# Gate and up of the FFN as seven block products for two batches, on one core

## What is computed

```python
x = L0_attn_hidden_states
x = x + attention(layernorm(x), w_attn, b_attn, w_proj, b_proj)
h = layernorm(x)
gate = silu(einsum('bsh,ih->bsi', h, w_gate))
up = einsum('bsh,ih->bsi', h, w_up)
return x + einsum('bsi,hi->bsh', gate * up, w_down)
```

## Time and profile before

| | |
|---|---|
| Median of 3 runs | 869.31 us (867.79 to 871.29) |
| Profiled execution | 872.76 us |
| Its span, first to last instruction | 871.1 us |
| Mean granted TensorE clock | 0.982 |
| Busy in the span | TensorE 816.1, VectorE 500.6, ScalarE 357.6, GpSimd 187.4 us |
| `ffn`, first matmul to end | 516.4 to 871.1 us |

### The profile page before, as it was taken

One profiled execution on the slowest core, in us unless ns is written; L12 is line 12 of the kernel. 1 busy time (PEld: TensorE's weight loads), 2 busy tenths in 40 slices (PEclk: granted clock), 3 DMA queues, 4 the chain that ended last, 5 costly groups with the idle time before them and its releaser, 6 DMA issues. The chain is left out here.

```text
span 871.1 us, 13365 instructions
## 1 busy us (share of the span) xinstructions
PE 816.1 (94%) x4576; PEld 563.4 (65%) x4576; DVE 500.6 (57%) x1539; ACT 357.6 (41%) x693; POOL 187.4 (22%) x336
## 2 busy tenths in 40 slices
PE   3889898999999999999978989999999999999998
PEld 3645365555555565565624668887888788878886
DVE  6598687887988779887784444342222312232223
ACT  4336566665666655666566323231111211121111
POOL 5224233343433424434234200000000000000000
PEclk9999899999999999999988989999999999999999
DMA  8864447565665556655642246004000400030001
GB/s 272 236 204 143 143 157 218 161 196 161 203 189 179 168 178 206 203 179 169 222 155 89 104 140 246 13 1 146 0 1 1 144 0 0 0 135 9 0 0 48
DMA packets 70563, 109.31 MB, mean 125 GB/s; under 512 B 13395, under 2 KB 38662, under 8 KB 70505
## 3 DMA queue, kind: packets, MB, share of 16 engines
q1 hardware_dynamic: 68457, 108.32, 38.9%
q10 hardware_dynamic: 2048, 0.27, 0.2%
HBM read 65.97 MB, written 42.32 MB: 124 GB/s over the span
## 5 line engine op out<-in xcount | busy, mean ns | idle before, releaser
L909 DVE CUSTOM_DVE_ANT_0 bank<-bank,mask_qk 128x512 f32<-128x512 f32 (+3 forms) x512 | 240.4, 514 | 56.3 <-PE bank L1148 53.9
L741 ACT ACTIVATE pt<-bank 128x512 f32<-128x512 f32 (+1 forms) x384 | 194.2, 529 | 136.9 <-PE bank L1170 123.3
L1170 PE MATMUL bank<-q_st,k_st 116*128 116x512 bf16 (+3 forms) x512 | 135.4, 308 | 15.9 <-ACT pt L741 13.2
L1148 PE MATMUL bank<-k_st,q_st 97*128 97x512 bf16 (+3 forms) x512 | 133.2, 311 | 10.8 <-DMA q_st<-slopes_dram 4.8
L1487 DVE TENSOR_TENSOR gu<-bank,silu 128x512 f32<-128x512 f32 x40 | 27.7, 692 | 200.6 <-issue 121.1
L1148 PEld LDWEIGHTS bank<-k_st,q_st 97*128 97x128 bf16 x512 | 41.5, 99 | 79.7 <-issue 39.9
L1265 PE MATMUL bank<-fT_hi,wgu_hi 128*128 128x512 f32 x224 | 88.5, 395 | 4.1 <-DVE wgu_lo L1457 4.1
L1265 PE MATMUL bank<-fT_lo,wgu_hi 128*128 128x512 f32 x224 | 88.2, 394 | 0.0
L1265 PE MATMUL bank<-fT_hi,wgu_lo 128*128 128x512 f32 x224 | 88.1, 393 | 0.0
L1420 ACT ACTIVATE silu<-bank 128x512 f32<-128x512 f32 x40 | 24.0, 600 | 148.2 <-PE bank L1265 148.2
L646 POOL TENSOR_SCALAR_AFFINE_SELECT pt<-pt 128x256 f32<-128x256 f32 x128 | 56.5, 442 | 129.7 <-ACT pt L741 129.7
(11 more groups left out here) (106 smaller groups left out, 1396.6 us busy)
## 6 DMA issues: line engine op xcount, KB each, us to landing
stack_dram<-scratch SPq DMA_DIRECT2D x32, 384.0 KB, 3.1
q_st<-stack_dram SPq DMA_DIRECT2D x32, 384.0 KB
k_st<-stack_dram SPq DMA_DIRECT2D x32, 384.0 KB
stack_dram<-scratch SPq DMA_DIRECT2D x32, 256.0 KB, 3.5
pv_dram<-weighed SPq DMA_DIRECT2D x32, 256.0 KB, 4.4
weighed<-pv_dram SPq DMA_DIRECT2D x17, 256.0 KB
xt<-x SPq DMA_DIRECT2D x16, 256.0 KB, 3.6
stack_dram<-scratch SPq DMA_DIRECT2D x32, 128.0 KB, 4.2
```

The costliest lines, as they stand in the source:

```text
L741: act.activation(pt[:, h % PT_RING, COL0[k]:COL0[k] + WIDE[k]], bank[3 + (3 * h + k) % 2][:, 0:WIDE[k]], ACT.Exp, scale=1.0 / HD).then_inc ...
L909: last = dve.tensor_tensor_reduce(bank[k][:, at:at + n], bank[k][:, at:at + n], mask_qk[:, S - n:S], 1.0, NEG, ALU.add, ALU.max, mx[:, h % ...
L1148: last = pe.matmul(bank[k][:, at:at + n], q_st[0:K_MAX, s, h % 4, t * P:(t + 1) * P], k_st[0:K_MAX, s, h % 4, 0:n], start=True, stop=True)
L1170: last = pe.matmul(bank[3 + u % 2][:, at:at + n], k_st[0:K_EXP, s, h % 4, t * P:(t + 1) * P], q_st[0:K_EXP, s, h % 4, t * P:S], start=True ...
```

## The change

Gate and up of one block for two batches are a product of 2x2 blocks: the weights' rows are gate and up, their columns the two halves of the contraction (A11, A12: gate; A21, A22: up), the tokens' rows the two halves, their columns the even and the odd batch (0 and 1, then 2 and 3). Eight block products become seven, by Winograd's scheme, with sums of weights S1 = A21 + A22, S2 = S1 - A11, S3 = A11 - A21, S4 = A12 - S2 and combinations T1 to T4 of the tokens. A *unit* (`unit(u)`, 17 of them in `UNITS`) makes the seven products P1, P2, P6, P5, P7, P3, P4 in this order, each of 2 halves x 3 passes = 6 matmuls, in four PSUM banks in turn, and the seven sums of products on VectorE. Even gate = P1 + P2; u2 = P1 + P6; u4 = u2 + P5; odd gate = P3 + u4; the new u2 = u2 + P7; odd up = P5 + u2; even up = P4 + u2.

- Units cover blocks 5 to 10 of batches 0 and 1 (pair 0, units 0 to 5) and blocks 0 to 10 of batches 2 and 3 (pair 1, units 6 to 16). Block 4 of batch 0 and blocks 0 to 4 of batch 1 stay plain products of 24 matmuls (`tile`, six of them in `TILES`).
- ScalarE copies P1 to SBUF (`p1`), since each sum reads one bank and one SBUF tile. It takes Silu of both gates, casts the unit's new weights (`weights_hi`), the weight sums (`weight_sums_hi`), the down weights (`down_hi`) and the even product (`product_hi`).
- GpSimd makes the four sums of weights of 128x256 for each unit (`weight_sums`) and the subtraction for each down weight (`down_lo`). VectorE makes the low parts of the weights in front (`weights_lo`, 512 and 256 columns) and of their sums (`weight_sums_lo`, 1024 columns) for the next unit, between its sums of products.
- Behind a unit's products TensorE works the four parts of an even down (`BEHIND`; unit 6 has none). The odd batch's products wait in SBUF (`gu_odd`); its ten remaining downs run in a row at the end of the pair (`END`), after down 10 (odd block 0) and down 11 (even block 10). Downs are numbered by `DOWNS`, 44 in all.
- Weights are no longer kept: down weights go through three raw and four split slots and are loaded and split for each of the 44 downs; gate and up weights through two raw slots, once for each unit and the first tile.
- Tokens of batches 2 and 3 are loaded in unit 0 and their statistics and normalisation follow in units 1 to 3; they are transposed in two rounds of 16 among the odd downs of pair 0, and combined block by block (`combine_round`). Tokens of batch 1 are transposed between downs 1 and 2. There is no fourth set of transposes.
- The loop over batches is written out.

The diff, cut to the lines that set the order and the costs (`sb` and `sem` declarations, SyncE's order at the pair's end, plain tiles and the removed loop bodies are left out):

```diff
+    RAW, RAW_DOWN, GU, WD = 2, 3, EARLY, 4
+    PLAIN = EARLY + 1
+    TILES = [(0, EARLY)] + [(1, f) for f in range(PLAIN)]
+    UNITS = [(0, f) for f in range(PLAIN, FT)] + [(1, f) for f in range(FT)]
+    FIRST = FT - PLAIN
+    DOWNS = [(0, f) for f in range(FT - 1)] + [(1, 0), (0, FT - 1)] + [(1, f) for f in range(1, FT)]
+    DOWNS += [(b + 2, f) for b, f in DOWNS]
+    PAIR = 2 * FT
+    BEHIND = {u: EARLY + u for u in range(FIRST)} | {u: PAIR + u - FIRST - 1 for u in range(FIRST + 1, len(UNITS))}
+    END = {FIRST - 1: FT, len(UNITS) - 1: PAIR + FT}
+    DOWN_BANK = ((0, 1, 2, 3), (7, 6, 4, 5), (4, 5, 6, 7), (2, 1, 3, 0))
...
+    P1, P2, P6, P5, P7, P3, P4 = range(7)
+    def product_bank(u, j):
+        return bank[4 + (7 * u + j) % 4] if u < FIRST else bank[(7 * (u - FIRST) + j) % 4]
...
+        def place(w, u):
+            at = u % 2 * 2 * 2 * KT * P
+            return w[:, at:at + 7 * 2 * P].rearrange("p (o k m) -> p o k m", o=7, k=2)
...
+            for u in range(len(UNITS)):
+                if u in BEHIND:
+                    load_down(BEHIND[u] + 2)
+                load_gate_up(RAW + 1 + u)
+                if u == 0:
+                    sp.wait_ge(c_lo, 4)
+                    load_tokens(2)
+                    for s in x1_stored:
+                        sp.wait_ge(s, B * TT // 2 * 16)
+                    load_tokens(3)
...
+            def weight_sums(u):
+                if u >= len(UNITS):
+                    return
+                need(pool, w_lo_done, 2 * u)
+                pool.wait_ge(raw_in[(u + 1) % RAW], 16 * ((u + 1) // RAW + 1))
+                raw = wgu_raw[(u + 1) % RAW]
+                s = {o: weight_sum[:, o - S1, :, :] for o in (S1, S2, S3, S4)}
+                a11, a12, a21, a22 = raw[:, 0, 0:2, :], raw[:, 0, 2:4, :], raw[:, 1, 0:2, :], raw[:, 1, 2:4, :]
+                pool.tensor_tensor(s[S1], a21, a22, ALU.add).then_inc(sum_step, 1)
+                pool.tensor_tensor(s[S3], a11, a21, ALU.subtract).then_inc(sum_step, 1)
+                pool.wait_ge(sum_step, 3 * u + 1)
+                pool.tensor_tensor(s[S2], s[S1], a11, ALU.subtract).then_inc(sum_step, 1)
+                pool.wait_ge(sum_step, 3 * u + 3)
+                pool.tensor_tensor(s[S4], a12, s[S2], ALU.subtract).then_inc(sums_made, 1)
...
+            for u in range(len(UNITS)):
+                weight_sums(u + 1)
+                if u in (2, 3):
+                    deviation(u)
+                if u in BEHIND:
+                    down_lo(BEHIND[u] + 1)
+                if u == FIRST:
+                    down_lo(PAIR)
+                if u in END:
+                    for n in range(END[u], END[u] + FT):
+                        down_lo(n)
...
+                raw, hi = wgu_raw[(u + 1) % RAW], place(w_hi, u)
+                act.copy(hi[:, A11:A12 + 1, :, :].rearrange("p o k m -> p (o k) m"), raw[:, 0, :, :])
+                act.copy(hi[:, A22, :, :], raw[:, 1, 2:4, :]).then_inc(w_hi_done, 1)
...
+                act.wait_ge(sums_made, u + 1)
+                act.copy(place(w_hi, u)[:, S1:S4 + 1, :, :], weight_sum[:, :, :, :]).then_inc(w_hi_done, 1)
...
+                act.wait_ge(t_done, KT + 4 * (r + 1))
+                act.copy(hT_hi[:, r, :], bank[0][:, :]).then_inc(t_hi, 1)
+                act.copy(oT[0][:, r, :], bank[1][:, :]).then_inc(t_hi, 1)
+                act.copy(hT_hi[:, r + 2, :], bank[2][:, :]).then_inc(t_hi, 1)
+                act.copy(oT[1][:, r, :], bank[3][:, :]).then_inc(t_hi, 1)
+                act.copy(oT_hi[r + 2], bank[3][:, :]).then_inc(t_hi, 1)
...
+            for u in range(len(UNITS)):
+                pair, f = UNITS[u]
+                act.wait_ge(product_done, 7 * u + P1 + 1)
+                need(act, summed, 7 * u - 5)
+                act.copy(p1, product_bank(u, P1)[:, :]).then_inc(copied, 1)
+                act.wait_ge(summed, 7 * u + 1)
+                act.activation(gates[:, 0, :], gates[:, 0, :], ACT.Silu).then_inc(silu_done, 1)
+                weights_hi(u + 1)
+                if u in BEHIND:
+                    down_hi(BEHIND[u] + 1)
+                if u == FIRST:
+                    down_hi(PAIR)
+                weight_sums_hi(u + 1)
+                if u in END:
+                    down_hi(END[u])
+                    product_hi(END[u] - 1)
+                act.wait_ge(summed, 7 * u + 6)
+                act.activation(gates[:, 1, :], gates[:, 1, :], ACT.Silu).then_inc(silu_done, 1)
+                product_hi(DOWNS.index((2 * pair, f)))
+                if u in END:
+                    for i in range(FT - 1):
+                        down_hi(END[u] + 1 + i)
+                        product_hi(END[u] + 1 + i)
+                        if pair == 0 and i in (3, 5):
+                            transposed_round((i - 3) // 2)
+                        if pair == 0 and i in (4, 6):
+                            round_combination_hi(i // 2 - 2)
...
+            def combine_round(r):
+                at = 2 * 3 + 4 * r
+                c1, c2, c3, c4 = [combination(1, j, r) for j in (T1, T2, T3, T4)]
+                dve.wait_ge(t_hi, 2 * KT + 5 * r + 5)
+                dve.tensor_tensor(c1, oT[0][:, r, :], bank[0][:, :], ALU.subtract).then_inc(combined, 1)
+                dve.tensor_tensor(c3, oT[1][:, r, :], oT[0][:, r, :], ALU.subtract).then_inc(combined, 1)
+                dve.wait_ge(combined, at + 1)
+                dve.tensor_tensor(c2, oT[1][:, r, :], c1, ALU.subtract).then_inc(combined, 1)
+                dve.wait_ge(combined, at + 3)
+                dve.tensor_tensor(c4, bank[2][:, :], c2, ALU.subtract).then_inc(combined, 1)
...
+                dve.wait_ge(product_done, 7 * u + P2 + 1)
+                dve.wait_ge(copied, u + 1)
+                dve.tensor_tensor(gates[:, 0, :], p[P2][:, :], p1, ALU.add).then_inc(summed, 1)
+                dve.wait_ge(product_done, 7 * u + P6 + 1)
+                dve.tensor_tensor(u2, p[P6][:, :], p1, ALU.add).then_inc(summed, 1)
+                dve.wait_ge(product_done, 7 * u + P5 + 1)
+                dve.wait_ge(summed, 7 * u + 2)
+                dve.tensor_tensor(u4, p[P5][:, :], u2, ALU.add).then_inc(summed, 1)
+                weights_lo(u + 1)
+                dve.wait_ge(product_done, 7 * u + P7 + 1)
+                dve.tensor_tensor(u2, p[P7][:, :], u2, ALU.add).then_inc(summed, 1)
+                dve.wait_ge(summed, 7 * u + 4)
+                dve.tensor_tensor(up_odd, p[P5][:, :], u2, ALU.add).then_inc(summed, 1)
+                dve.wait_ge(product_done, 7 * u + P3 + 1)
+                dve.tensor_tensor(gates[:, 1, :], p[P3][:, :], u4, ALU.add).then_inc(summed, 1)
+                weight_sums_lo(u + 1)
+                if u in (2, 3):
+                    normalised(u)
+                if u in (1, 2):
+                    token_statistics(u + 1)
+                if u in END:
+                    product_lo(END[u] - 1)
+                dve.wait_ge(silu_done, len(TILES) + 2 * u + 2)
+                dve.tensor_tensor(gu_odd[:, f, :], gates[:, 1, :], up_odd, ALU.mult).then_inc(odd_done, 1)
+                dve.wait_ge(product_done, 7 * u + P4 + 1)
+                dve.tensor_tensor(u2, p[P4][:, :], u2, ALU.add).then_inc(summed, 1)
+                dve.wait_ge(summed, 7 * u + 7)
+                dve.tensor_tensor(gu_even[:, :], u2, gates[:, 0, :], ALU.mult).then_inc(even_done, 1)
+                product_lo(DOWNS.index((2 * pair, f)))
+                if u in END:
+                    for i in range(FT - 1):
+                        product_lo(END[u] + 1 + i)
+                        if i == 0:
+                            add_residual(2 * pair)
+                        if pair == 0 and i in (3, 5):
+                            round_lo((i - 3) // 2)
+                        if pair == 0 and i in (3, 5):
+                            combine_round((i - 3) // 2)
+                        if pair == 0 and i in (4, 6):
+                            round_combination_lo(i // 2 - 2, 0)
+                            round_combination_lo(i // 2 - 2, 1)
+                        if pair == 0 and i in (5, 7):
+                            round_combination_lo((i - 5) // 2, 2)
+                            round_combination_lo((i - 5) // 2, 3)
...
+                    pe.wait_ge(out_ready, TT)
+                else:
+                    pe.wait_ge(t_hi, 2 * KT + 5)
+                    pe.wait_ge(t_lo, KT + 3)
+                    pe.wait_ge(combined, 6 + 4)
...
+                exact_product(pe, product_bank(u, j), [(w[:, o, k, :], v[:, o, k, :], x_hi[:, k, :], x_lo[:, k, :])
+                                                       for k in range(2)]).then_inc(product_done, 1)
...
+                pe.wait_ge(w_lo_done, 2 * u + 1)
+                need(pe, summed, 7 * u - 2)
+                block_product(u, P1, A11, hT_hi[:, 0:2, :], hT_lo[:, 0:2, :])
+                block_product(u, P2, A12, hT_hi[:, 2:4, :], hT_lo[:, 2:4, :])
+                if u == 0:
+                    pe.wait_ge(odd_done, 5)
```

(84 more changed lines are left out.)

516 lines of the change are left out of this document (297 added, 219 removed).

## The result

The changed kernel takes 863.7 us in the median (859.3 to 868.0, 14 runs), the kernel before 869.3 in the same comparison; the ratio is 0.9932, 95% interval 0.991 to 0.9953. It is faster by 5.6 us where 15 were forecast. The direction came out, and so did the gains and the place of the two largest waits; what the new work on GpSimd and VectorE costs did not.

The account below looks back on a forecast made before the run. TensorE's matmuls were taken to bound `ffn`. Gains of 26.8 us (23.1 matmuls, 1.75 transposes, 2.0 waits) less costs of 11.8 gave 15.0 net, so a median of 854.3 from 869.3; range 845 to 864.

Parts of the forecast that it names:

- Unit 1: Token statistics of 3.05 us ahead of `product_lo` put it at 18.1 against 16.3: a TensorE wait of 1.8 us.
- The port in a plain unit: GpSimd's sums hold up VectorE once, 0.65 us; `product_lo` ends at 15.6, slack 0.7, no stall; bounds 0 to 2.6.
- (b): Rival: port lock by all four GpSimd sums in every unit, 18 to 27 us, median 872 to 881; chance 0.08.
- (c): Rival: two to three port meetings per unit, 0.6 x 14 = 8.4 us, median 863; chance 0.12.
- Unit 2: Normalisation (1.92) and statistics, 4.97 us together, put `product_lo` at 20.0: a TensorE wait of 3.65 us.
- Unit 3: Normalisation ahead of `product_lo` makes TensorE wait 0.85 us.
- at the slow clock unit 3's 0.85 is covered: One clock fall after unit 2's wait costs 3.05 us; unit 3's 0.85 then drops out. Bounds 0 to 9.
- Downs around the end of batch 0's units: End of pair 0: down 11 late by 0.85, transposes between odd downs 0.65, later casts and combinations at down 18 0.3.
- Unit 7: Unit 6 has no down, 9.52 us against 9.2 of VectorE work, so the next part 0 is 0.3 late.
- The three waits (2.0) go: Waits at the starts of batches 1 to 3, for transposed tokens, vanish because these are ready long before: 2.0 us gained.
- Restarts: Matmuls behind a wait run slower: 0.3 us for about seven waits, less three old ones, 1.2 us.
- The tail stays: Last matmul to end stays 4.4 us; the last sums wait only for TensorE, 0.16 sooner.

Follow-up runs that it names:

- small_sums: Changed kernel with GpSimd's four sums of weights cut to 2 of 128 columns from unit 1 on; stage 342.9 us, 5.5 less than the changed kernel.
- small_pool: small_sums with the low parts of the down weights also cut to 2 of 512 columns from the fifth on; stage 336.9 us, 11.5 less than the changed kernel.
- late_sums: Changed kernel, GpSimd's sums made to wait until the even block's `product_lo` is done; 856.65 us median, ratio 0.9845 to the kernel before.
- memset_sums: Changed kernel with GpSimd's four sums replaced from unit 1 on by four zero fills, which read nothing; stage 349.2 us against 348.4.
- no_tokens: Changed kernel without the token work of units 1 to 3, except one small operation in each of two units; stage 338.6 us against 348.4.
- late_spread: Changed kernel with late_sums and spread_tokens together, and `product_lo(10)` moved ahead of the weights' low parts; 849.56 us median, ratio 0.9767 to the kernel before.
- spread_tokens: Changed kernel, token work spread in single operations over units 1 to 5, batch 3's normalisation moved to the odd downs' start; stage 338.0 us against 348.4.

## Why the prediction was wrong

The steps that failed are prices of the sum, and most of them have one root. The prediction let GpSimd's sums meet VectorE once in a plain unit and nowhere else: in the stalls it took every VectorE operation at its time alone (the normalisation at 1.92, `product_lo` among the odd downs at 0.69). Measured, they meet twice in each plain unit, four normalisations take 3.10, and `product_lo` of an odd block takes 1.17. The second failure is unit 3, whose wait the sum put at nothing.

The ledger by stage lengths, from the starts of the matmuls. Gains: 23.1 for the 102 matmuls and 1.75 for the transposes, as forecast; the old pass starts 0.65 + 0.94 + 0.92 = 2.5; the start of the stage 1.1, luck; and the tail 1.1, which nobody had forecast. Together 29.6. Costs: waits 18.3, two stretches at the slow clock in units 2 and 3 3.3, plain units 0.7, restarts 0.9 (each wait makes the second matmul behind it some 0.08 late; those of the kernel before are taken off). Net 6.4, measured 6.3.

- **Right:** what bounds the kernel, the work removed and its pace (18 matmuls in 4.08), the start and the downs of pair 1 covered, the waits behind units 1 and 2 with their cause and place, a slow stretch after unit 2. Unit 1 came to the tenth (1.8), partly by luck: 1.5 of it is there without the sums (small_sums).
- **The port in a plain unit** was taken as one meeting and slack 0.7. It is two: in the timeline GpSimd's second sum begins 0.07 ahead of the even product and its fourth 0.06 ahead of `product_lo`, and `product_lo` ended 16.1 after its unit's start, not 15.6. The bound (four meetings) was stated, and the price per meeting was near (0.65 forecast, 0.5 measured). Plain units lost 0.09 each in the mean, so rivals (b) and (c) did not come, but the margin was gone for every unit with anything extra.
- **Unit 2:** 4.8 for 3.65. The step that failed is "normalisation 1.92": it took 3.10 beside GpSimd's sums, in unit 2 and in unit 3, and 1.91 with the sums cut to two columns (small_sums).
- **Unit 3:** two steps failed. By the prediction's own numbers the wait was 15.0 + 1.92 - 16.3 = 0.6, not 0.85; with the normalisation at 3.10 and the odd product held too (1.23 for 0.68, at 622.82) it comes to 2.4, which is what was measured. And "at the slow clock unit 3's 0.85 is covered" did not hold: the slow stretch ended at 614.4, ahead of P7 and P3, and `product_lo` follows on P3's sum, so the stretch put off both sides alike. The clock fell again behind this wait. The two stretches lost 1.6 and 1.7, where one of 3.05, like that of the start, was forecast, so the sum for the clock was right by chance.

```profile
622.82 1.23 DVE L1777 TENSOR_TENSOR gu_odd<-gates,sums 128x512 f32<-128x512 f32 x1
```

- **Downs around the end of batch 0's units:** 1.2 for down 10, where I had `product_lo(10)` in time, 0.6 for down 11 where I had 0.85, and in the odd downs of pair 0 1.2 + 0.3 + 2.25 + 0.6 for 0.65 + 0.3. I had priced each VectorE operation alone though GpSimd subtracts down weights all the time there; `product_lo` took 1174 ns in the mean for odd blocks, and 687 with next to no GpSimd work beside it (small_pool).
- **Unit 7:** 1.8 for 0.3; with late_sums 0.7. That rest is the order's own: unit 6 ends in 9.52, and `product_lo` has then to come within 9.52 + 4.08 = 13.6 of its start, which it did not with next to no sums either (small_sums 0.8).
- **"The three waits (2.0) go":** the passes' starts gave 2.5, but three ends of a batch cost 0.5 each in the kernel after. TensorE waits there for its own last matmul (`sum_done`) before it raises `down_done`; no run took this wait out. I had put the whole of the old waits down to the transposes. 1.5 us of the shortfall.
- **Restarts:** 1.2 forecast; 0.9 in the ledger, with another 0.16 for each of 13 waits counted in the waits above.
- **"The tail stays":** it became 1.1 us shorter. In the kernel before, the fourth set of transposes, which feeds nothing, also stood ahead of the last additions on VectorE: their low parts (L1479) ran to 865.81 and the additions (L1510) behind them, though the first bank was summed by 864.7. In the kernel after, the additions (L1723) follow TensorE alone. From the start of the last matmul (866.34 before, 860.70 after) to the end are 4.7 and 3.7 us.

```profile
863.33 2.48 DVE L1479 TENSOR_TENSOR fT_lo<-bank,fT_hi 128x512 fp32r<-128x512 f32 x4 [1.65 <-ACT fT_hi L1414]
...
859.15 2.66 DVE L1723 TENSOR_TENSOR x<-bank,x 128x512 f32<-128x512 f32 x4 [6.32 <-PE bank L1854]
...
860.70 0.39 PE L1854 MATMUL bank<-wd_hi,w_lo 128*128 128x512 f32 x1
```

The range (845 to 864) held the 863.7 at its edge; the point was off by 9.4 in the medians and, in the stage lengths, by 15.0 - 6.3 = 8.7. These are units 2 and 3 with 3.6, downs 10 and 11 and the odd downs 4.3, unit 7 1.5, batch ends 1.5, plain units 0.7 and the slow stretches 0.2, together 11.8, less the start 1.1, the tail 1.1, the pass starts 0.5 and the restarts 0.3.

## What to carry to other kernels

When a change gives GpSimd real work beside a VectorE that feeds the critical engine, take as the upper price of each VectorE operation on two SBUF tiles, and of each normalisation, its time alone plus the GpSimd operation that it can meet. Sums with one input in PSUM stayed at 0.69 us here. Look at what releases the two engines: if it is the same moment, they meet every time. One wait that moves GpSimd's sums beside sums out of PSUM (late_sums) took 6.0 us off the stage, about as much as the whole change (6.3). Serial side work belongs in the idle pieces of a unit, not behind its last input: spread out in single operations the same work left waits of some 1.3 us where it had cost 9.0 and two slow stretches.

## What the runs showed of the hardware that I had not expected

- A VectorE normalisation (two per-partition scalars, 128x512 in float32) went from 543 ns alone to 1109 in the mean of memset_sums, with fills by GpSimd beside most of them, while operations on two SBUF tiles of the even blocks stayed at 692; beside GpSimd sums, which read, the latter went to 1.2 us.
- In the kernel after, the granted clock fell behind TensorE's waits of 4.8 and 2.4 us (units 2 and 3), and each time some 1.6 us was lost, where the start of the stage in the kernel before lost 2.9 by the same measure. The length of the wait alone does not decide it: the wait of 2.2 us at down 19 was followed by the slow clock in small_sums, no_tokens and late_spread, and by the full clock in after, memset_sums, late_sums and spread_tokens. Behind it, in after and then in late_spread (us, TensorE busy, granted clock, DMA share, GB/s):

```profile
683.50:686.50 3.00, 2.99 (x12) 1.00 0.31 126
...
666.50:669.50 3.00, 3.00 (x8) 0.54 0.38 150
```

- At the same place of the code, the start of the stage, the first 24 matmuls took 7.05 to 8.4 us from start to start in ten profiled executions.
